# Two small gate operations move from VectorE to ScalarE in a gated mLSTM block with a spiking MLP

## The reference

```python
ig = (ifg @ igate_w.T + igate_b).T            # ifg = [q, k, v]
fg = (ifg @ fgate_w.T + fgate_b).T
cs = jnp.cumsum(jax.nn.log_sigmoid(fg), axis=1)
log_D = where(tril, cs[:, :, None] - cs[:, None, :], -inf) + ig[:, None, :]
max_log_D = jnp.max(log_D, axis=-1, keepdims=True)
C = qk * jnp.exp(log_D - max_log_D)
normalizer = jnp.maximum(jnp.abs(C.sum(-1)), jnp.exp(-max_log_D))
h = (C / (normalizer + EPS)) @ vh             # then a layer norm and a scale
x = x + tanh(g_xattn) * h
...
h = square(relu(layernorm(x) @ W_fc.T))       # 256 -> 1024
y = h @ W_proj.T                              # 1024 -> 256
# five steps of a threshold unit on y count spikes
x = x + tanh(g_ffn) * spikes / 5
```

## Time and profile before

| | |
|---|---|
| median of 3 runs | 672.32 us (671.55 to 674.33) |
| the profiled execution's own time | 670.95 us |
| its span in the trace | 669.2 us |
| granted TensorE clock, mean | 0.983 |
| busy share: PE, DVE, ACT, POOL | 89%, 81%, 73%, 73% |

### The profile page before, as it was taken

One profiled execution on the slowest core, in us unless ns is written; L12 is line 12 of the kernel. 1 busy time (PEld: TensorE's weight loads), 2 busy tenths in 40 slices (PEclk: granted clock), 3 DMA queues, 4 the chain that ended last, 5 costly groups with the idle time before them and its releaser, 6 DMA issues.

```text
span 669.2 us, 17636 instructions
## 1 busy us (share of the span) xinstructions
PE 594.2 (89%) x6032; PEld 487.7 (73%) x6032; DVE 542.0 (81%) x1218; ACT 488.9 (73%) x1014; POOL 486.9 (73%) x535
## 2 busy tenths in 40 slices
PE   1364688799999999999999999999999999999795
PEld 0253577687787877888778878887788777787684
DVE  5567768888998899899989998989988898968522
ACT  5565557777887887887887887788778877686463
POOL 5374568769797979977897789797978788675232
PEclk9999989989999999999999999999999999999988
DMA  7584442963259166735575529734580555300000
GB/s 194 130 195 110 90 90 90 143 140 72 75 147 205 34 128 114 198 45 97 137 181 99 96 80 169 171 64 98 138 207 14 108 99 137 73 2 32 1 31 33
DMA packets 73192, 71.33 MB, mean 107 GB/s; under 512 B 8720, under 2 KB 68752, under 8 KB 73104
## 3 DMA queue, kind: packets, MB, share of 16 engines
q1 hardware_dynamic: 71984, 70.02, 47.0%
q10 hardware_dynamic: 1120, 0.18, 0.3%
HBM read 27.44 MB, written 8.39 MB: 54 GB/s over the span
## 4 chain that ended last, share of the span: by engine, by line
PE 55%; issue 12%; ACT 10%; POOL 10%; DVE 10%; DMA 1%; SPq 1%; ACTq 0%; POOLq 0%; DVEq 0%
PE y_ps L1048 17%; PE z_ps L988 16%; POOL sq_lo L1031 4%; PE qk_ps L708 3%; PE arg_ps L693 3%; PE misc_ps L461 3%; PE misc_ps L527 3%; POOL c_lo L737 2%; DVE spikes L1066 2%; ACT sq_hi L1010 2%; PE pv_ps L832 2%; PE pv_ps L757 2%; PE pv_ps L755 1%; PE pv_ps L756 1%; POOL am_rest L635 1%
## 5 line engine op out<-in xcount | busy, mean ns | idle before, releaser
L1031 POOL TENSOR_TENSOR sq_lo<-w_raw,sq_hi 128x512 fp32r<-128x512 f32 (+1 forms) x96 | 112.6, 1174 | 70.7 <-ACT w_raw L1011 68.3
L737 POOL TENSOR_TENSOR c_lo<-decay 128x512 bf16<-128x512 f32 x128 | 132.2, 1040 | 11.2 <-DVE decay L727 11.0
L988 PE MATMUL z_ps<-x_hi,wfc_hi 128*128 128x512 f32 (+1 forms) x288 | 116.2, 403 | 5.1 <-ACT relu L998 2.5
L1048 PE MATMUL y_ps<-sq_hi,wpr_hi 128*128 128x512 f32 (+1 forms) x288 | 116.1, 403 | 2.0 <-POOL sq_lo L1031 1.9
L1048 PE MATMUL y_ps<-sq_lo,wpr_hi 128*128 128x512 f32 (+1 forms) x288 | 107.6, 374 | 0.0
L1048 PE MATMUL y_ps<-sq_hi,wpr_lo 128*128 128x512 f32 (+1 forms) x288 | 107.5, 373 | 0.0
L988 PE MATMUL z_ps<-x_hi,wfc_lo 128*128 128x512 f32 (+1 forms) x288 | 107.5, 373 | 0.0
L988 PE MATMUL z_ps<-x_lo,wfc_hi 128*128 128x512 f32 (+1 forms) x288 | 107.4, 373 | 0.0
L727 DVE TENSOR_TENSOR decay<-qk_ps,decay 128x512 f32<-128x512 f32 x128 | 86.8, 678 | 21.4 <-PE qk_ps L708 17.1
L719 ACT ACTIVATE decay<-arg_ps,lqk_col 128x512 f32<-128x512 f32 x128 | 86.4, 675 | 23.5 <-PE arg_ps L696 22.7
L1031 POOL TENSOR_TENSOR sq_lo<-relu,sq_hi 128x512 fp32r<-128x512 f32 (+1 forms) x48 | 56.0, 1168 | 44.3 <-ACT relu L1011 41.6
(11 more groups left out here) (138 smaller groups left out, 1694.5 us busy)
## 6 DMA issues: line engine op xcount, KB each, us to landing
x_in<-x SPq DMA_DIRECT2D x32, 256.0 KB, 3.0
v_in<-ctx_rows SPq DMA_DIRECT2D x32, 256.0 KB, 3.3
kT_in<-ctx_cols SPq DMA_DIRECT2D x32, 256.0 KB, 3.7
k_stack<-kT_hi SPq DMA_DIRECT2D x64, 128.0 KB, 3.3
k_stack<-kT_lo SPq DMA_DIRECT2D x64, 128.0 KB, 3.6
q_stack<-qT_hi SPq DMA_DIRECT2D x64, 128.0 KB, 3.9
q_stack<-qT_lo SPq DMA_DIRECT2D x64, 128.0 KB, 4.3
out<-w_raw SPq DMA_DIRECT2D x32, 256.0 KB, 3.5
```

Source lines behind the costliest of these rows:

```text
L737: e.tensor_tensor(c_lo[i % NCH][:, :], c, top(c), ALU.subtract).then_inc(sem("c_lo"), 1)
L988: ins = e.matmul(z_ps[:, tokens(q)], lhsT, rhs, start=(n == 0), stop=(n == len(terms) - 1))
L1031: e.tensor_tensor(sq_lo[n % NSQ][:, tokens(q)], relu[n % NRE][:, tokens(q)], sq_hi[n % NSQ][:, tokens(q)].bitcast(fp32), ALU.subtract).the ...
L1048: ins = e.matmul(y[:, c, :], w[:, j, c * P:(c + 1) * P], h, start=(j == 0 and i == 0 and (c == 0 or whole)), stop=(j == FT - 1 and i == 2) ...
```

## The change

Two operations leave VectorE's list and come back on ScalarE's; the wait of `floor_T` grows by one semaphore.

```diff
 def gate_softplus(e, g):        # ScalarE
+    e.activation(i_pre[0:r, :], misc_ps[0:r, 0:S], ACT.Identity, bias=gate_bias[0:r, 0:1])
     ins = e.activation(f_log[0:r, :], misc_ps[0:r, S:2 * S], ACT.Abs, bias=gate_bias[0:r, 1:2])
     ins.then_inc(sem("gate_abs"), 1)
...
 def gate_pre(e, g):             # VectorE
-    e.tensor_scalar(f_neg[0:r, :], misc_ps[0:r, S:2 * S], gate_bias[0:r, 1:2], 0.0, ALU.add, ALU.min)
-    e.tensor_scalar(i_pre[0:r, :], misc_ps[0:r, 0:S], gate_bias[0:r, 0:1], None, ALU.add).then_inc(sem("gT_free"), 1)
+    e.tensor_scalar(f_neg[0:r, :], misc_ps[0:r, S:2 * S], gate_bias[0:r, 1:2], 0.0, ALU.add, ALU.min).then_inc(sem("gT_free"), 1)
...
 def gate_cummax(e, g):          # VectorE
-    top = m[:, P - 1:P]
-    e.tensor_scalar(cs[0:r, 0:P], a[:, 0:P], -1.0, top, ALU.mult, ALU.add)
-    e.tensor_scalar(cs[0:r, P:S], m[:, P:S], top, None, ALU.subtract).then_inc(sem("gate_cummax"), 1)
+    e.tensor_scalar(cs[0:r, P:S], m[:, P:S], m[:, P - 1:P], None, ALU.subtract).then_inc(sem("gate_cummax"), 1)
+
+def gate_ends(e, g):             # ScalarE
+    e.wait_ge(sem("gate_cummax"), g + 1)
+    e.activation(cs[0:r, 0:P], am[0:r, 0, 0:P], ACT.Identity, bias=am[0:r, 1, P - 1:P], scale=-1.0).then_inc(sem("gate_ends"), 1)
...
 def floor_T(e, g):              # TensorE
     e.wait_ge(sem("gate_cummax"), g + 1)
+    e.wait_ge(sem("gate_ends"), g + 1)
...
 # scalar_program, for every group
     am_split(e, g, 0)
+    gate_ends(e, g)
     ...
```

More of the change, by code:

```diff
@@ L610, in gate_cummax @@
             link(e, "vector", e.tensor_tensor(row_max[0:r, :], m, cs[0:r, :], ALU.add))
-            top = m[:, P - 1:P]
-            e.tensor_scalar(cs[0:r, 0:P], a[:, 0:P], -1.0, top, ALU.mult, ALU.add)
-            e.tensor_scalar(cs[0:r, P:S], m[:, P:S], top, None, ALU.subtract).then_inc(sem("gate_cummax"), 1)
+            e.tensor_scalar(cs[0:r, P:S], m[:, P:S], m[:, P - 1:P], None, ALU.subtract).then_inc(sem("gate_cummax"), 1)
+        def gate_ends(e, g):
+            if not 0 <= g < NG:
+                return
+            e.wait_ge(sem("gate_cummax"), g + 1)
+            r = group_rows(g)
+            e.activation(cs[0:r, 0:P], am[0:r, 0, 0:P], ACT.Identity, bias=am[0:r, 1, P - 1:P], scale=-1.0).then_inc(sem("gate_ends"), 1)
         def am_split(e, g, n):
@@ L1180, in scalar_program @@
             am_split(e, 0, 0)
+            gate_ends(e, 0)
             am_split(e, 0, 2)
@@ L1188, in scalar_program @@
             am_split(e, 1, 0)
+            gate_ends(e, 1)
             decay_exp(e, 0, 0)
@@ L1213, in scalar_program @@
             am_split(e, 2, 0)
+            gate_ends(e, 2)
             decay_exp(e, 1, 2)
@@ L1252, in scalar_program @@
             am_split(e, 3, 0)
+            gate_ends(e, 3)
             square(e, 0, 5)
@@ L1339, in scalar_program @@
                 am_split(e, n + 3, 0)
+                gate_ends(e, n + 3)
                 decay_exp(e, 4 * n + 3, 2)
```

## The result

The changed kernel took 674.94 us (median of 21 runs, 673.81 to 682.25), the kernel before, run beside it on the same chip, 673.12 us (21 runs, 670.33 to 676.63). The ratio is 1.0051, with an interval of 1.0033 to 1.0068: some 3.4 us slower (2.2 to 4.6), which is the line between "no change" and "slower" that the prediction had drawn. That ratio does not come from the two medians, which lie only 1.8 us apart: the means are 676.36 and 673.04 us, 3.3 apart, and the lowest runs 3.5. Eleven of the changed kernel's runs lie between 673.81 and 674.94, the other ten between 676.60 and 682.25; no trace here shows why. The profiled execution took 674.17 us, span 672.4.

The account below looks back on a forecast made before the run. ScalarE, with instructions end to end for seven microseconds of every slot at the gates, was taken as the bound. 2.2 us (six slots) plus 1.2 (start-up) gave +3.4 on 672.32: 675.7 us, range 671.5 to 679.

Parts of the forecast that it names:

- The Identity: Head of ScalarE's unbroken gate stretch: the added instruction costs 0.37 us a group (0.32 to 0.50), which stays in the slot.
- Six slots, 2.2 us: The six large groups of the slots, 4 to 9: each pays the Identity's 0.37 us, together 2.2 us.
- VectorE before the scan: Removing the bias operation gains nothing: the scan also waits for ScalarE's Ln and starts 0.17 us later.
- The second `cs` write inherits the wait: VectorE behind the scans: the remaining write waits for GpSimd instead, taking about 1.2 us where it took 0.27.
- `gate_ends`: The `cs` write added on ScalarE: 0.30 us, 0.20 with overlap, hidden in 1.43 us of idle time behind `decay_exp`.
- `floor_T`'s wait: TensorE behind `state`: `gate_ends` ends at least 0.5 us before it is needed, so the new wait costs nothing.
- The start-up, +1.2: Groups 0 to 3: +0.1, +0.57, +0.37 and +0.20 us from the added ScalarE instructions, together 1.2 us.
- Hidden after all: Rival, chance 0.23: ScalarE's delay is taken up between 457.9 and 469.6 us; only start-up pays, 673.5, or nothing, 672.3.
- both on the path: Rival, chance 0.12: both added ScalarE instructions delay each slot, 0.82 us each, +6.8 in all, 679.1 us.
- VectorE is the one that matters: Rival, chance 0.10: relieving VectorE brings gate results and TensorE's `state` earlier, at most down to 669.9 us.
- I take 0: VectorE's hand-back after the gate work: between 0.05 us earlier and 0.17 later, taken as no shift.

Follow-up runs that it names:

- e1: The kernel before with only the input gates' bias Identity moved to ScalarE, both `cs` writes kept on VectorE: gate stretch 23.64 us, ratio 1.0065.
- e3: The changed kernel with a second, spare Identity ahead of the first on ScalarE: gate stretch 24.12 us, ratio to the kernel before 1.0128.
- e12: e7 with a spare Identity put ahead of ScalarE's Exp: gate stretch 23.30 us, ratio to the kernel before 0.9982.
- e5: The kernel before with one more PSUM operation on VectorE, into spare rows: gate stretch 24.27 us, ratio 1.0124.
- e2: The kernel before with only `gate_ends` (first-half `cs` write) moved to ScalarE, plus `floor_T`'s wait: gate stretch 23.30 us, ratio 1.0027.
- e10: The kernel before with only `ln2_rstd` put ahead of `x2_hi_step` on ScalarE: gate stretch 23.28 us, ratio 0.9984.
- e8: The kernel before with one of VectorE's four third-layer-norm offsets (L372) in a slot left out: gate stretch 23.07 us, ratio 0.9976.
- e4: The kernel before with both `cs` writes moved to ScalarE, plus a small negating copy, bias left on VectorE: gate stretch 23.27 us, ratio 1.0028.
- e9: e5 with the same layer-norm offset left out as in e8: gate stretch 23.64 us, ratio to the kernel before 1.0035.
- e7: The kernel before without the Abs (Exp straight from PSUM) and with `ln2_rstd` ahead of `x2_hi_step`: 667.53 us, ratio 0.9944.

## Why the prediction was right

**The time.** The forecast was 675.7 us, the measured median is 674.94 and inside the range; the +3.4 us met the ratio's 3.4. Of these, 2.2 are shown in the slots. The other 1.2 are a remainder, and that it equals the term for the start-up is at least in part luck: the medians (1.8 us apart) would leave nothing for it.

**The Identity: right.** Predicted 0.37 a slot, on the path in full; measured 0.35 to 0.36 in the stretch in each of six groups, and 71.71 from Identity to Identity against "about 71.7". e1 has all of it, e3 shows that the place charges each instruction its spacing. "Six slots, 2.2 us" is 6 x 0.36 = 2.2. The exact 0.37 owes something to luck. It rests on independent instructions overlapping by 0.10 us; so they do here, Identity to Abs, but the second Identity of e3 and the Exp of e12 did not overlap at all. That pair would have cost 0.48, still within the 0.32 to 0.50 given.

**VectorE before the scan: right.** The scan starts 457.30 - 455.51 = 1.79 us behind the transposes' end ("some 1.8"), and L587's old time is idle time.

**The second `cs` write inherits the wait: right.** L612 takes 1.27 us, and VectorE's gate work ends at 460.89, 5.34 behind ScalarE's first gate instruction where it was 5.39 (5.38 and 5.41 behind the transposes' end): 0.03 to 0.05 earlier, the edge of the range given (0.05 earlier to 0.17 later). Removing the instruction that was blocked moved the wait to the next one, L614's 0.27 us to L612's 1.27. The Trainium skill ("SBUF — State Buffer", "Who interferes with whom") states that a VectorE instruction with two SBUF inputs contends with a GpSimd instruction that reads SBUF. The traces agree: `row_max` took 1.34 us in e5, against 0.41 in the change, and L373 1.71.

**`gate_ends`: hidden as said, a little mis-sized.** It takes 0.386 us and 0.30 of spacing, where I had 0.30 and 0.20. The idle time behind it went from 1.43 to 1.13, not to 1.2, and hid all but 0.03 of it (e2). `floor_T`'s wait cost nothing that I can find: in group 8 L621 ends at 462.97, `floor_T` starts at 463.78 behind `state`, and the kernel's stretch is not longer than e1's.

**The start-up, +1.2: not shown by the profiles, and the total doesn't contradict it.** Up to sequence 6 the profiled execution lay 2.27 us behind that of before, and from its last `inter` to the end it made up 1.5. TensorE's granted clock differs in both parts. At the end (600 to 640 us) it is 0.98 after the change and 0.91 before. Windows of 50 to 90 us in the kernel before, the change and e2 (columns as in the earlier trace rows):

```profile
50.00:90.00 40.00, 23.10 (x291) 20.06 (x292) 27.54 (x64) 22.91 (x53) 20.73 (x24) 0.96 0.44 97
```

```profile
50.00:90.00 40.00, 22.45 (x285) 19.52 (x286) 27.58 (x62) 21.32 (x51) 19.44 (x22) 0.66 0.40 94
```

```profile
50.00:90.00 40.00, 25.09 (x255) 21.97 (x256) 26.45 (x61) 19.25 (x45) 18.95 (x21) 0.50 0.45 94
```

The clock is 0.96, 0.66 and 0.50, the last being the 1.2 GHz level throughout. All three come out of 50 us in which TensorE was busy for less than 20 and the clock stood at 1.00. e2, which has nothing to pay there but 0.20 for a group, was 3.4 us late at sequence 2. But the mean clock of this window doesn't settle it: in e10, whose lists are those of before up to there, it is 0.70, and its first `inter` of sequence 2 comes 0.04 us from that of before, where that of the change is 1.89 late. So how much of the 2.27 is the clock's, and how much the added instructions', is open. Nor does the stretch ahead of the clock's fall tell: the first `inter` of all, at 44.48 us before, comes 0.55 later in the change, but 0.59 earlier in e8, whose lists are the same to there as those of before. A single profile can't tell 1.2 us in such a stretch. The timed runs can, roughly: the change's 3.4 us less the slots' 2.2 leave 1.2 (0 to 2.4). e3 and e5 leave more outside the slots: 6 x 0.85 = 5.1 and 6 x 1.00 = 6.0 in the slots, 8.6 (7.1 to 10.0) and 8.3 (6.0 to 10.8) in all. That the two halves alone (e1 4.4 and e2 1.8 us) add up to more than the whole is at the edge of their intervals, and I leave it open.

**The rivals.** "Hidden after all" is excluded by the stretch, "both on the path" by e2 and by the idle time left. "VectorE is the one that matters" was refused in its own direction by e4, but e5 and e9 show that I dismissed it too quickly: the prediction read VectorE as beside the path, and in the kernel before it has only 0.18 us to spare ahead of L372 and 0.20 over `x_lo`. In the changed kernel, which the prediction was about, there is more: VectorE idles 0.57 us ahead of L372, and 12.3 us lie between `z_step` and `inter`, which need 11.7. Had the handed-over wait ended at the upper end of my range, 0.17 later, these rows say that it would have cost nothing. So "I take 0" was right, though the prediction had not worked out the room that it rests on.

## What to carry to other kernels

Before moving work between engines, find the stretch in which it stands and ask which engine's instructions stand end to end there; the mean busy shares said VectorE, the place said ScalarE, and the place was right to 0.01 us. Test a "beside the path" in both directions, and look for the engine's smallest idle time ahead of an instruction that others wait for: VectorE was worth nothing when 1.3 us early and cost 1.00 us when 0.57 late, with 0.2 us to spare. Removing work from the bound engine pays only until the next chain (here 0.27 of 0.50 us). To shorten a chain, see whether an instruction can be taken out of it by algebra, rather than hand work to it from a neighbour: e7 did that, and its ratio of 0.9944 is below those of the kernel before and of the change.

## What had not been expected of the hardware

- **A short instruction blocked twice.** A VectorE operation on 128x2 elements took 0.13 to 0.15 us alone, 1.03 when it met one of GpSimd's instructions near that one's start, and 1.71 when it met two. In e5 GpSimd started its next instruction (470.72) while VectorE's had been waiting since 470.06.
- **Spacing on ScalarE depends on the pair.** Behind an Identity of 0.47 us the Abs started after 0.37, a second Identity or an Exp after 0.48, all from PSUM and independent of one another. Why was not tried.
- **Single slots that are long.** e5's gate stretch was 27.79 us in group 7 against 24.27 in the others, e4's 26.71 in group 6 (and 24.22 in its group 7). In the two long ones VectorE waited for a load of `x_in`, for 2.0 and 2.6 us. The wait of e5 in 378 to 388 us (total, times, longest):

```profile
DVE stat L357 <- DMA x_in<-x: 2.0, 1, 2.0
```

Such groups are single ones of some profiled executions, and they are why the medians of six groups stand in the table and not the spans.
